# Two-layer graph network: layer two with a fixed number of row chunks for each target tile, sums kept in PSUM, and target rows expanded from three bf16 parts

## The reference, cut to what matters

```
msg_in    = concat(x[src], x[dst])                 # 512 wide, one row per edge
messages  = relu(msg_in @ W_msg + b_msg)           # 256 wide
aggregated = segment_sum(messages, dst)            # 12,500 rows
h = relu(concat(x, aggregated) @ W_upd + b_upd);  out = layernorm(x + layernorm(h) * gamma + beta)
```

## Time and profile before

| | |
|---|---|
| median of 3 runs | 4493.01 us (4489.8 to 4494.67) |
| profiled execution, span | 4487.7 us |
| PE / PEld busy | 3872.0 us (86%) / 3230.9 us (72%) |
| DVE / ACT / POOL busy | 3447.3 (77%) / 2775.7 (62%) / 2768.4 us (62%) |
| mean granted TensorE clock | 0.937 |

### The profile page before, as it was taken

How to read it: one execution, slowest core, us unless ns; L and a number is a source line. 1 busy time by engine, 2 the same in 40 slices (tenths; PEclk the granted TensorE clock), 3 DMA queues, 4 the chain that set the end, 5 groups by cost and what they waited for, 6 DMA issues and landing times.

```text
span 4487.7 us, 86383 instructions
## 1 busy us (share of the span) xinstructions
PE 3872.0 (86%) x26503; PEld 3230.9 (72%) x26503; DVE 3447.3 (77%) x7772; ACT 2775.7 (62%) x7163; POOL 2768.4 (62%) x2817
## 2 busy tenths in 40 slices
PE   4999999899999999975888887887888788788886
PEld 3999999788888888854666666666666666666665
DVE  7999999799999999964666666666666666666665
ACT  3777777777777777753555555655555555555554
POOL 2887999644454455426666666666666666666662
PEclk9999999999999999987898989999888899998898
DMA  4776444567777777743444444444444444444443
GB/s 126 234 220 221 179 174 173 189 191 201 206 206 206 207 206 206 207 146 114 128 136 133 130 134 129 137 134 129 134 135 134 127 140 131 129 138 132 134 123 72
DMA packets 345349, 710.35 MB, mean 158 GB/s; under 512 B 58425, under 2 KB 201606, under 8 KB 344866
## 3 DMA queue, kind: packets, MB, share of 16 engines
q0 software_dynamic: 115680, 361.28, 30.3%
q1 hardware_dynamic: 229218, 343.52, 22.5%
HBM read 510.45 MB, written 195.74 MB: 157 GB/s over the span
## 4 chain that ended last, share of the span: by engine, by line
PE 53%; DVE 18%; issue 14%; another core or an unknown queue 11%; DVEq 2%; ACT 1%; SPq 1%; DMA 1%; POOL 0%; ACTq 0%; POOLq 0%
PE ps L1307 19%; PE ps L1329 10%; PE ps L1341 9%; DVE big L1901 7%; DVE arena L1911 4%; PE ps L1289 2%; PE ps L1145 2%; PE ps L1155 2%; PE ps L1362 1%; PE ps L1364 1%; DVEq L1901 1%; DVE big L1608 1%; PE ps L1140 1%; DVE small L1918 1%
## 5 line engine op out<-in xcount | busy, mean ns | idle before, releaser
L800 POOL DMA_INDIRECT arena<-d_p,tabs x1628 | 1558.1, 957 | 892.4 <-issue 457.6
L1329 PE MATMUL ps<-arena 128*128 128x256 f32 x3256 | 911.1, 421 | 238.1 <-DVE big L1901 179.9
L1911 DVE TENSOR_TENSOR arena<-arena,ps 128x512 f32<-128x512 f32 x814 | 531.2, 682 | 756.7 <-remote 535.1
L1111 ACT ACTIVATE arena<-arena 128x1024 f32<-128x1024 f32 x407 | 429.9, 1056 | 1017.4 <-DVE arena L1911 958.8
L1341 PE MATMUL ps<-big,scr 128*128 x3256 | 849.9, 402 | 241.1 <-DVE arena L1911 165.7
L1329 PEld LDWEIGHTS ps<-arena 128*128 128x128 f32 x3256 | 642.4, 207 | 438.8 <-ACT arena L1111 210.8
L1341 PEld LDWEIGHTS ps<-big,scr 128*128 128x128 f32 x3256 | 649.6, 203 | 378.2 <-issue 281.1
L786 POOL DMA_INDIRECT arena<-d_m,scr x392 | 530.9, 1354 | 578.5 <-DVE arena L1754 253.0
L1901 DVE SCALAR_TENSOR_TENSOR big<-big,tabs,ps 128x256 f32 x1628 | 773.6, 475 | 108.8 <-DVE big L1901 51.7
L1307 PE MATMUL ps<-arena,scr 128*128 128x256 f32 x2620 | 609.7, 383 | 2.3 <-DVE arena L1754 2.3
L1307 PEld LDWEIGHTS ps<-arena,scr 128*128 128x128 f32 x2620 | 487.9, 190 | 68.1 <-issue 2.9
(11 more groups left out here) (285 smaller groups left out, 6049.4 us busy)
## 6 DMA issues: line engine op xcount, KB each, us to landing
d_m<-arena SPq DMA_DIRECT2D x108, 603.0 KB
arena<-d_loc SPq DMA_DIRECT2D x136, 384.0 KB
d_m<-arena SPq DMA_DIRECT2D x108, 402.0 KB
arena<-d_p,tabs POOLq DMA_INDIRECT x1628
arena<-in_xT_dram SPq DMA_DIRECT2D x96, 256.0 KB
d_xp<-arena SPq DMA_DIRECT2D x49, 256.0 KB, 3.2
arena<-d_xp SPq DMA_DIRECT2D x49, 256.0 KB
d_x<-arena SPq DMA_DIRECT2D x49, 256.0 KB
```

The source lines that it names most:

```text
L800: e.indirect_dma_start(out=G1[j % 8][:, k, :], out_offset=None, in_=d_p, in_offset=bass.IndirectOffsetOnAxis(ap=tabS[:, j, k:k + 1], axis= ...
L1111: e.activation(G1[g % 8], G1[g % 8], ACT.Relu).then_inc(S("f_re"), 1)
L1329: m = e.matmul(turn(H, AB)[:, k * 256:k * 256 + 256], OH1[(j - 2) % 4][:, 2 * h + k, :], G1[(j - 2) % 8][:, 2 * h + k, :], start=True, sto ...
L1911: e.tensor_tensor(v, v, q2(turn(2 * j + h, QB)[:, :]), ALU.add).then_inc(S("f_m"), 1)
```

## The change

Every tile now has PERT = 17 chunks whether or not its edges fill them, and the last tile 12, so there are 97 x 17 + 12 = 1,661 chunks in 416 groups, and the tile of a chunk is known when the program is built. `trow`, the register loads, the mask `has`, table `tabK` and its four blocks, and most of the counting chain go. The sums of a tile's 17 chunks accumulate in PSUM (`SB`, two banks, one for each pair), and ACT copies a finished pair to `SM` once. Q is kept for six pairs (`Q3`) as three bf16 parts, high, middle and low; DVE and ACT split it. `OT1` becomes bf16, and the expansion of a chunk is three bf16 products with the same one-hot matrix. `QB` grows from 3 half groups to 5. `node1` has one step more.

```diff
+PERT = 17
+LASTC = 12
+NCH = 97 * PERT + LASTC
+NG = -(-NCH // 4)
-FIRSTS = [(2, c0, min(c0 + 4, NC)) for c0 in range(0, NC, 4)]
+def tile_of(n):
+    return min(n // PERT, NT - 1)
...
-LAST_ROW = [33 * (p + 1) + 11 for p in range(NP)]
+LAST_ROW = [min(2 * PERT * (p + 1), NCH) - 1 for p in range(NP)]
-FIRST_F = [-(-n // 4) + 3 for n in LAST_ROW]
-F_STEPS = 18
+FIRST_F = [n // 4 + 3 for n in LAST_ROW]
+F_STEPS = 19
...
-        OT1 = [take(4, 128) for _ in range(2)]
+        OT1 = [b16(take(256)).rearrange("p (a b) -> p a b", a=4) for _ in range(2)]
-        QB = PS[0:3]
-        AB = PS[3:7]
+        QB = PS[0:3] + PS[5:7]
+        SB = PS[3:5]
+        Q3 = [b16(take(768)).rearrange("p (b i n) -> p b i n", b=2, i=3) for _ in range(QR)]
+        SM = [take(2, 256) for _ in range(2)]
+        RQ = take(2, 256)
...
             def gath(j, g, i):
                 waitn(e, "f_ag", 2 * (j - 7))
-                for k in range(4):
+                for k in range(min(4, NCH - 4 * j)):
...
# ACT
                 if o == 18 and p < QL:
-                    e.activation(big[:, 2 * p + 1:2 * p + 3, :], q2(PS[3][:, :]), ACT.Copy).then_inc(S("b_pq"), 1)
+                    e.activation(Q3[p % QR][:, :, 0, :], q2(PS[3][:, :]), ACT.Copy).then_inc(S("b_pq"), 1)
+                if o == 20 and p < QL:
+                    waitn(e, "b_qr", p + 1)
+                    e.activation(Q3[p % QR][:, :, 1, :], RQ, ACT.Copy).then_inc(S("b_qm"), 1)
...
+                if o == 0:
+                    waitn(e, "f_ag", LAST_ROW[p] // 2 + 1)
+                    waitn(e, "g_tr", p - 1)
+                    e.activation(SM[p % 2], q2(SB[p % 2][:, :]), ACT.Copy).then_inc(S("g_sc"), 1)
+                if o == 7 and p + QL < NP:
+                    waitn(e, "g_qm", p + 1)
+                    e.activation(Q3[(p + QL) % QR][:, :, 0, :], q2(PG[:, :]), ACT.Copy).then_inc(S("g_qc"), 1)
+                if o == 9 and p + QL < NP:
+                    waitn(e, "g_qr", p + 1)
+                    e.activation(Q3[(p + QL) % QR][:, :, 1, :], RQ, ACT.Copy).then_inc(S("g_qh"), 1)
...
# PE
-                    for h in range(2):
-                        H = 2 * (j - 2) + h
-                        waitn(e, "f_acc", 2 * (H - 3))
-                        for k in range(2):
-                            m = e.matmul(turn(H, AB)[:, k * 256:k * 256 + 256], OH1[(j - 2) % 4][:, 2 * h + k, :],
-                                         G1[(j - 2) % 8][:, 2 * h + k, :], start=True, stop=True)
-                        m.then_inc(S("f_ag"), 1)
+                    for n in range(4 * (j - 2), min(4 * (j - 1), NCH)):
+                        t, k = tile_of(n), n % 4
+                        first, end = (n == PERT * t), (n == NCH - 1 or tile_of(n + 1) > t)
+                        if first and t % 2 == 0:
+                            waitn(e, "g_sc", t // 2 - 1)
+                        m = e.matmul(SB[t // 2 % 2][:, t % 2 * 256:t % 2 * 256 + 256], OH1[(j - 2) % 4][:, k, :],
+                                     G1[(j - 2) % 8][:, k, :], start=first, stop=end)
+                        if n % 2 == 1 or n == NCH - 1:
+                            m.then_inc(S("f_ag"), 1)
                 if j < NG:
-                    e.load(regs, four(trow, j))
-                    ts = [e.snap(r, min_val=0, max_val=NT - 1) for r in regs]
                     waitn(e, "f_ot", j + 1)
-                    waitn(e, "g_qc", ahead(j))
-                        waitn(e, "f_m", H - 2)
-                            m = e.matmul(turn(H, QB)[:, k * 256:k * 256 + 256], OT1[j % 2][:, 2 * h + k, :],
-                                         big[:, ts[2 * h + k] + 1, :], start=True, stop=True)
+                    waitn(e, "g_ql", ahead(j))
+                            waitn(e, "f_m", H - 4)
+                        for i in range(3):
+                            m = e.matmul(turn(H, QB)[:, n % 2 * 256:n % 2 * 256 + 256], OT1[j % 2][:, k, :],
+                                         Q3[t // 2 % QR][:, t % 2, i, :], start=(i == 0), stop=(i == 2))
...
# DVE
-                    e.scalar_tensor_tensor(big[:, ts[k], :], big[:, ts[k], :], tabK[:, j - 3, k:k + 1],
-                                           turn(H, AB)[:, (k % 2) * 256:(k % 2) * 256 + 256],
-                                           ALU.mult, ALU.add).then_inc(S("f_acc"), 1)
+                if o == 8 and p + QL < NP:
+                    waitn(e, "g_qc", p + 1)
+                    e.tensor_tensor(RQ, q2(PG[:, :]), Q3[(p + QL) % QR][:, :, 0, :], ALU.subtract).then_inc(S("g_qr"), 1)
+                if o == 10 and p + QL < NP:
+                    waitn(e, "g_qh", p + 1)
+                    e.tensor_tensor(Q3[(p + QL) % QR][:, :, 2, :], RQ, Q3[(p + QL) % QR][:, :, 1, :], ALU.subtract).then_inc(S("g_ql"), 1)
```

More of the change, by code:

```diff
@@ L162 @@
 QL = 4
-SPAN = 11
+QR = 6
 AT_F = placed(FIRST_F, F_STEPS, {NP - 4: (8, 2), NP - 3: (0, 2), NP - 2: (0, 3)})
@@ L323, in grid @@
             return v.rearrange("p (a b) -> p a b", b=n)
-        tabN, tabS, tabK = (grid(tabs[:, k * NGT * 4:(k + 1) * NGT * 4], 4) for k in range(3))
+        tabN, tabS = (grid(tabs[:, k * NGT * 4:(k + 1) * NGT * 4], 4) for k in range(2))
         tabS = tabS.bitcast(i32)
@@ L396, in gnn @@
         ri = take(1).bitcast(i32)
[L397 to L400, removed]
+        st, dC = (take(100) for _ in range(2))
+        cS, tfl = (take(NC) for _ in range(2))
+        cI = take(NC).bitcast(i32)
         dbi = take(NB).bitcast(i32)
@@ L1316, in _ @@
             waitn(e, "b_pq", pq(NP, 0))
-            e.wait_ge(s_At, len(TABS + FIRSTS))
-            regs = [e.alloc_register(f"pet{k}") for k in range(4)]
+            waitn(e, "b_ql", QL)
+            e.wait_ge(s_At, len(TABS))
             def edge1(j):
@@ L1741, in _ @@
             assert n[0] == T_DONE
-            e.wait_ge(s_tl, 32)
-            e.wait_ge(S("e_z"), 1)
-            regs = [e.alloc_register(f"dvt{k}") for k in range(4)]
             def ready(g):
@@ L1913, in node1 @@
+                    for h in range(0, n, 2):
+                        w = min(2, n - h)
+                        H = 2 * j + h // 2
+                        waitn(e, "f_qe", H + 1)
+                        v = G1[j % 8][:, h:h + w, :]
+                        e.tensor_tensor(v, v, q2(turn(H, QB)[:, :])[:, 0:w, :], ALU.add).then_inc(S("f_m"), 1)
             def node1(p, o):
                 u = UH[p % 3]
-                if o in (5, 12):
-                    waitn(e, "g_re" if o == 5 else "g_add", p + 1)
+                if o in (6, 13):
+                    waitn(e, "g_re" if o == 6 else "g_add", p + 1)
@@ L2103, in constants @@
     c[:, C_PID] = p
-    c[:, C_STEP:C_STEP + NC] = p[:, None] + 128 * np.arange(NC, dtype=np.float32)[None, :]
+    rows = np.arange(128)[:, None] + 128 * np.arange(NC)[None, :]
+    tile = np.where(rows < NCH, np.minimum(rows // PERT, NT - 1), NT)
+    c[:, C_TIL:C_TIL + NC] = tile
+    c[:, C_OFF:C_OFF + NC] = np.where(rows < NCH, 128 * (rows - PERT * tile), 0)
     c[:, C_DUMP] = NROW + p
```

218 lines of the change are left out of this document (77 added, 141 removed).

## The result

The changed kernel takes 4506.93 us (median of 6 runs, 4496.36 to 4510.34), the kernel before 4491.41 us beside it (6 runs, 4486.98 to 4494.91): ratio 1.0033, 95% interval 1.0022 to 1.0044. It is slower by 15.5 us; 4515 had been forecast. The profiled executions differ by 4504.2 - 4487.7 = 16.5 us.

What follows compares the result with a forecast made beforehand. Layer two was taken as bound by gathers at about 1.44 us each; 47 (gathers) - 7 (pauses) - 12 (counting chain) - 1 (layer one) - 5 (tail) = +22 us, so 4515 us, range 4430 to 4560.

Steps and rivals of the forecast that it cites:

- The price of a gather: Layer two: each gather costs 1.25 + 0.75/4 = 1.44 us whatever PE and DVE do; 33 more gathers, +47 us.
- The law of the pauses: POOL in layer two: a pause lasts about 0.23 + 0.75 us for each group issued in the run before it.
- The pauses: POOL in layer two: runs grow from 1.83 to 2.2 groups, giving 189 pauses, 32 fewer, -7 us.
- The head: Before the first gather: shorter counting chain on DVE in the first stage, -12 us, and layer one, -1 us.
- The tail: From last gather to end, 70 us: PE's 6.7 us wait for the adds shrinks; -5 us, bounds 0 and -12.
- the signs named: Layer two: gathers 1.25 us apart with pauses, DVE under half busy, products at 0.11 us, first to last gather 2440 to 2455.
- Rival B: Layer two: PE hands on five or more groups in a run, so pauses are fewer; 4425 to 4484 us; chance 0.18.
- Its break-even: Layer two under long runs: no change overall at 1.43 us a gather and fewer than 60 pauses.
- Rival C: Layer two: pauses get worse or `fits` locks POOL, delaying 360 gathers; +60 us, 4575 us; chance 0.09.
- Rival A: Layer two: late signals go, POOL never pauses, gathers' issue is the only floor; -330 us, about 4145 us; chance 0.12.
- the reading behind the forecast: Layer two: PE's signals come late while POOL streams gathers, until a backlog growing with the gathers drains; chance 0.60.

Runs made afterwards that it cites:

- stretches 1, 4, 5 and 7: Parts of one run of the changed kernel: as is; one product a chunk; POOL four groups ahead; adds put back: 1.470, 1.507, 1.463, 1.482 us a gather.
- stretches: Changed kernel with layer two in eight parts of 52 groups, each varying gather issue or engine work; 0.964 (plain transfers) to 1.564 us a gather.
- bextra: Kernel before with 414 groups in layer two instead of 407, 28 more gathers, the last seven groups with empty rows: 4174.27 us, ratio 1.0127.
- noadds: Kernel before with DVE's adds of layer two and PE's waits for them left out: 4103.18 us, ratio 0.9953.
- again: Changed kernel unchanged, on another chip beside the kernel before: 4120.33 us against 4120.94, ratio 0.9997.

## Why the prediction was right, and where it was mis-sized

**The price of a gather: right for the chip of the profile.** "1.44 us whatever PE and DVE do", with 0.23 us for a pause: the whole came to 1.478 us before and 1.480 after, and stretches 1, 4, 5 and 7 give 1.46 to 1.51 with the engines' work changed both ways. It isn't exact: with three gathers a group it was 1.56, not 1.48. The law of the pauses holds for runs of 4 to 12 only: in stretches, 5 runs of 16 gathers were followed by 3.10 us on average, where it says 3.53, and the first 36 gathers by 6.15 in the kernel before, where it says 7.28. The seven more groups of bextra, the direct test of the price, ran on a chip without pauses and cost 53 us, not 35, so on a chip with pauses the price rests on the stretches and on the sum above.

**The pauses: mis-sized.** Runs grew from 1.83 groups to 1.97, not to 2.2, and 11 pauses fell away (221 to 210), not 32. Gathers and pauses were to cost +40 and cost +52. Runs of four have longer pauses than before (1.54 against 1.29), so fewer pauses did not make less: their sum is 419 us in both.

**The head: right.** The first gather starts 12.3 us sooner; the sum had 13. Line 1684, line 1707 of the kernel before, opens the second stage in both:

```profile
L1684 DVE TENSOR_SCALAR scr<-scr x98: 341/346/536, 854.0 to 1916.5; 108x512 f16<-108x512 f16 x98
```

It starts at 854.0 us, 864.2 before: the first stage is 10.2 us shorter, where 12 had been taken. The second gives the other 2.1, where 1 had been.

**The tail: mis-sized, -5 against -22.9**, outside its own bound of -12. The bound was PE's recorded wait in the sum products (6.7 us) alone. It left out the transposes behind the adds, 4.61 us in one wait, and that groups close up when neither adds nor f32 expansions stand between them (3.04 us apart). The two errors, 12 and 18 us, largely cancel, so the closeness of 4507 to 4515 is in part luck. The direction does not hang on it: with the measured head and middle and the forecast's own tail of -5 the change would have cost 34 us. Of the signs named, the time from first to last gather, 2456.9 us, lies just above the 2440 to 2455; DVE under half busy and products at 0.11 us came as said.

**Rival B** (long runs) did not come. Its break-even was also mis-stated: with the prediction's own terms, layer two may cost 2406 + 18 us, and at 1.4375 us a gather that leaves room for some 90 pauses, not 60. **Rival C** did not either. `fits` in the changed kernel (shortest, median and longest duration):

```profile
L1864 DVE TENSOR_SCALAR scr<-arena,cstb x416: 344/347/591, 2004.4 to 4479.2; 128x512 bf16<-128x512 bf16 x139
```

It takes 347 ns, as its 16-bit neighbour did, and gathers took 0.960 us on average against 0.957. The average hides a small effect. The 383 gathers that lie beside a `fits` take 0.979 us and the others 0.955, 9 us in sum. In the kernel before the 406 beside one took 0.954 and the others 0.958, but in noadds, with `fits` still in f32, it is 0.977 and 0.951, so this does not hang on the 16-bit form. A lock of GpSimd for the whole of `fits`, as the Trainium skill ("SBUF — State Buffer", "Who interferes with whom") describes it for the two-port modes, shows in no row here; by it the gathers would have been up to 146 us longer in sum.

**Rival A, and the reading behind the forecast.** "Signals from PE come late while POOL streams gathers" holds on the chip of the first profiles and two others, in part: PE's and DVE's own issue stalls as well. On three other chips the same gathers at the same 1.25 us disturb nobody, in either kernel. There the change costs 33 x 1.259 = +42 us of gathers, gives back 11 at the head (first gather 2010.99 in noadds, 1999.68 in again), and the rest, 31 us, makes it even: 0.9997. The adds' 18 us are among that rest; the other 13 are not assigned. The forecast of "slower" was right for one kind of chip and would have been wrong on the other, where nothing changed. Nothing in a single profile could tell that. What differs between the chips stays open: packets, gathers, and the first two stages look alike. So does the mechanism: the traces show that the engines stand still while indexed gathers are issued, not what they stand still for.

No version that computes the whole beat both kernels. On a chip without pauses the floor is the number of gathers, and the tiles' fixed 17 chunks are what set it; on one with pauses spacing the gathers out to 1.53 us won nothing.

## What to carry to other kernels

Where POOL issues indexed gathers back to back, price a stage by their number first: 1.25 us of POOL for each 128 rows here, of 1 KB or of 512 bytes, and 1.48 in all on the chips with pauses. Work taken off the other engines under that cover is worth only what it saves ahead of the first gather and behind the last, and 2% more gathers ate all of it here. Read the head and the tail wait by wait, for that is where the gain is, and bound it by every wait there, not by one line's. And a price made of pauses is a price of one chip: look at a second before building on it.

## What the runs showed of the hardware

- The kernel before takes 4121 to 4126 us on three chips and 4491 to 4502 on two others and on that of the first profiles, with the runs of one kernel on one chip within 0.4%. The difference lies in layer two: its first gather starts at 2010 to 2012 us on either kind.
- On the slower ones, while indexed gathers are issued 1.25 us apart, PE issues products that wait for nothing one at a time, up to 1.6 us apart, and DVE and ACT show stalls of up to 7.6 and 9.6 us with no cause in the records. With plain transfers by the same engine, or where POOL pauses for 12 us, it ends; at a mean 1.53 us between gathers POOL no longer waits, but the engines are still held to 5.6 us a group.
- A gather of 128 rows of 1 KB and of 512 bytes costs POOL the same, 0.96 us and a gap of 0.30. Half of the gap can be used: two memsets (0.17 us) in it moved the median spacing by 0.01 us.
- A plain transfer of 128 rows by POOL takes it 0.54 us, a little over half of a gather.
